# Attention and a mixture-of-experts layer: in each expert's turn GpSimd issues the adds into the output ahead of the fetches of rank rows for the next expert

## The reference

```python
x = x + _L0_xattn_ref(_layernorm(x), ctx_1024, Wq, Wk, Wv, Wp, bp)     # 16 heads of 16
x = x + _L0_ffn_ref(_layernorm(x), ...)

# _L0_ffn_ref, cut: 8192 tokens, E = 16 experts, F = 1024, capacity 512 tokens per expert
xn = xf / rms * norm_weight
logits = xn @ router_weight.T + router_bias
probs = softmax(logits, axis=-1)
_, idx = top_k(logits.T, 512)                  # each expert picks its own 512 tokens
xe = xn[idx]
h = gelu(einsum('ecd,efd->ecf', xe, fc1_weight) + fc1_bias[:, None, :])
y = einsum('ecf,edf->ecd', h, fc2_weight) + fc2_bias[:, None, :]
gates = take_along_axis(probs.T, idx, axis=1)
output = zeros.at[flat_idx].add(y * gates[:, :, None])
gate_sums = zeros.at[flat_idx].add(gates)
output = where(gate_sums > 0, output / gate_sums, output)
```

## Time and profile before

| what | value |
|---|---|
| median of 3 runs | 1093.96 us (1087.89 to 1103.24) |
| profiled execution | 1097.2 us, its span 1095.2 us |
| PE busy | 886.7 us (81%) |
| DVE busy | 767.9 us (70%) |
| POOL busy | 645.6 us (59%) |
| ACT busy | 498.9 us (46%) |
| mean granted TensorE clock | 0.904 of full |

### The profile page before, as it was taken

The page is one execution under the profiler, slowest core; times in us unless marked ns, Lnnn a source line. Parts: engine busy times, 40 slices in busy tenths (PEclk is TensorE's granted clock), DMA queues, the critical chain, the costliest instruction groups (busy, mean ns, idle before and its releaser), DMA issues.

```text
span 1095.2 us, 20141 instructions
## 1 busy us (share of the span) xinstructions
PE 886.7 (81%) x6006; PEld 703.1 (64%) x6006; DVE 767.9 (70%) x1539; ACT 498.9 (46%) x868; POOL 645.6 (59%) x617
## 2 busy tenths in 40 slices
PE   4899999999999999997400015999999899989975
PEld 3566666766677666664400014888878798978874
DVE  4668888888888888875399885576666667676541
ACT  1446555556555565554100004564655544445440
POOL 3246655656656566553630055578887788888624
PEclk9889999999999999998555557999999999999996
DMA  4345555555565555552300052155555555555523
GB/s 157 134 143 186 194 209 210 186 207 189 192 218 192 196 199 184 212 213 99 109 0 0 0 156 85 39 134 141 152 157 149 134 133 129 134 137 131 125 63 38
DMA packets 110819, 155.17 MB, mean 142 GB/s; under 512 B 21180, under 2 KB 78780, under 8 KB 110784
## 3 DMA queue, kind: packets, MB, share of 16 engines
q1 hardware_dynamic: 94400, 133.71, 35.4%
q0 software_dynamic: 16384, 21.02, 10.8%
HBM read 61.86 MB, written 26.21 MB: 80 GB/s over the span
## 4 chain that ended last, share of the span: by engine, by line
PE 12%; DVE 11%; DMA 9%; issue 9%; POOL 8%; ACT 1%; SPq 0%; DVEq 0%; POOLq 0%; ACTq 0%
DMA W<-w1T_dram 4%; PE bank L1388 4%; PE bank L1389 4%; PE bank L1390 4%; DMA XG<-xn_table,II 3%; POOL XG L1075 2%; POOL out_dram L1101 2%; POOL RK L1069 2%; POOL G L1081 1%; DVE junk L883 1%; DVE before L1176 1%; DVE W2L L1221 1%; ACT W1H L1338 1%; DMA RK<-rank_table,RI 1%; DVE cand L893 1%
## 5 line engine op out<-in xcount | busy, mean ns | idle before, releaser
L525 DVE TENSOR_REDUCE NM<-bank 128x4 f32<-128x480 f32 x256 | 159.6, 656 | 53.7 <-PE bank L635 53.3
L368 ACT ACTIVATE PT<-bank 120x512 f32<-120x512 f32 x256 | 139.1, 595 | 64.4 <-PE bank L660 63.6
L310 POOL TENSOR_SCALAR XN<-X,mv,rstd 128x256 f32<-128x256 f32 x128 | 155.7, 1224 | 6.9 <-POOL rstd L305 6.1
L1388 PE MATMUL bank<-W2H,HH 128*128 128x256 f32 x512 | 147.5, 288 | 5.7 <-DVE Y L1261 5.7
L1389 PE MATMUL bank<-W2L,HH 128*128 128x256 f32 x512 | 145.9, 285 | 0.0
L1390 PE MATMUL bank<-W2H,HL 128*128 128x256 f32 x512 | 145.8, 285 | 0.0
L1247 DVE TENSOR_TENSOR HL<-HF,HH 128x512 fp32r<-128x512 f32 x128 | 87.0, 692 | 75.0 <-ACT HH L1351 74.8
L1101 POOL DMA_INDIRECT out_dram<-C,IO x60 | 112.1, 1868 | 45.0 <-DVE C L1266 27.3
L1388 PE MATMUL bank<-XTH,W1H 128*128 128x512 f32 x256 | 105.2, 411 | 18.7 <-DVE XTL L1231 18.7
L343 POOL TENSOR_TENSOR XB<-X,bp_sb 128x512 f32<-128x512 f32 x32 | 40.5, 1266 | 123.4 <-DVE X L536 123.4
L478 DVE RECIPROCAL RR<-RC 128x256 f32<-128x256 f32 x64 | 111.2, 1741 | 1.5 <-DMA RC<-PVS 1.5
(11 more groups left out here) (148 smaller groups left out, 1773.4 us busy)
## 6 DMA issues: line engine op xcount, KB each, us to landing
QX<-QH SPq DMA_DIRECT2D x64, 256.0 KB
W<-w1T_dram SPq DMA_DIRECT2D x16, 1024.0 KB
W<-w2T_dram SPq DMA_DIRECT2D x16, 1024.0 KB
KX<-KH SPq DMA_DIRECT2D x64, 240.0 KB, 2.3
X<-x_dram SPq DMA_DIRECT2D x32, 256.0 KB, 2.8
QX<-QL SPq DMA_DIRECT2D x32, 256.0 KB
RC<-PVS SPq DMA_DIRECT2D x32, 256.0 KB, 2.4
OC<-PVS SPq DMA_DIRECT2D x32, 256.0 KB, 2.6
```

The lines of the kernel that those rows point to most:

```text
L310: ins = pool.tensor_scalar(dst[:, t, :], src[:, t, :], mv[:, t, 0:1], rstd[:, t:t + 1], ALU.subtract, ALU.mult)
L368: act.activation(PT[u][0:M, HE * k:HE * (k + 1), :], score_bank[k % 2][0:M, :], ACT.Exp, scale=SCALE) \
L525: dve.tensor_reduce(NM[u][:, t, :].rearrange("p (f n e) -> p n e f", n=HN, e=HE)[:, n, :, :], smax_bank[q % 2][:, 0:4 * M].rearrange("p (e ...
L1388: pe.matmul(o, wh, xh, start=first, stop=False)
```

## The change

In both halves of GpSimd's loop the call of `add_up` changes place with the call of `ranks`. The loop's contents, its semaphores and the code before and behind it stay as they are.

```diff
@@ -1123,11 +1123,11 @@
         ranks(1, 1, RI[1])
         with pool.Fori(1, E // 2 - 1) as i:
             gather(i, 1)
+            add_up(i - 1, 0, False)
             ranks(i + 1, 0, RI[0])
-            add_up(i - 1, 0, False)
             gather(i + 1, 0)
+            add_up(i - 1, 1, False)
             ranks(i + 1, 1, RI[1])
-            add_up(i - 1, 1, False)
         gather(E // 2 - 1, 1)
         add_up(E // 2 - 2, 0, False)
         add_up(E // 2 - 2, 1, False)
```

## The result

The changed kernel took 1165.16 us (median of 4 runs, 1159.88 to 1166.56) against 1093.72 us (4 runs) before: ratio 1.0635, 95% interval 1.0552 to 1.0718. Two later comparisons of the same pair, on chips 4 and 5, gave 1.0474 (1.0411 to 1.0537) and, with more executions, 1.0584 (1.0558 to 1.0610). It is slower by 5 to 6%. The ratios leave out the few executions that ran over 1.5% above the fastest of their kernel. The forecast was 1139 us; the profiled execution took 1165.9 us, its span is 1163.9 us.

A forecast was written before the change was run, and what follows sets the result against it. GpSimd's queue was taken as the bound, TensorE close behind. Twelve waits of 3.7 us less 0.7 gave 43.7; plus 3.1, less 2.14 in the tail, 44.7, taken as +45: 1139 us, range 1117 to 1172.

The forecast's parts named there:

- forecast case: Likeliest case, each turn exposing the wait for rank rows: +45 us, 1139 us, own range 1126 to 1152, chance 0.72.
- rank rows that land late: Rival: rank rows take up to 8.2 us instead of 2.5; 1207 us, or 1162 in one turn of three; chance 0.12.
- GpSimd's queue bounds the turn: In the expert phase, GpSimd's 16 transfers a turn sum to 25.3 us against turns of 25.67; TensorE next at 24.3.
- The exposed chain: Rank fetch landing 2.48, `find` 1.59, GpSimd's reaction 0.90: 4.97 us, against 1.25 without a wait; new wait 3.7 a turn.
- the row of the phase's start: Expert phase's start, where VectorE really waited for rank rows: fetch issued at 646.11 us, `find` at 648.59, so 2.48 us.
- Twelve turns: Token fetches of experts 4 to 15 each follow a rank fetch directly: 12 x 3.7 - 0.7 = 43.7 us.
- the stretching: Lengthening of GpSimd instructions beside W1L, priced as unchanged when W1L meets rank fetches instead of adds.
- My layout: Predicted new turn, laid out from the first token fetch, to check that VectorE is free when rank rows land.
- G + 6.8: Time in us after G, the turn's first token fetch, near which W2L was predicted to end.
- The tail: After the last token fetch: 3.1 us later since `find` of expert 15 loses its lead, less a vanished 2.14 us wait.
- The clock: Rival: 5 us TensorE pauses slow first-layer matmuls, losing 10 us a turn; TensorE becomes the bound, 1199 us; chance 0.06.
- hidden: Rival, not slower: TensorE sets the pace, GpSimd's durations are only stretched, so the edit is hidden; 1094 us, chance 0.10.

The follow-up runs named there:

- The shortened HL: VectorE's HL subtraction done on 64 of 512 columns: changed kernel 1168.97 us, ratio 1.0494 to the kernel before; same edit in the kernel before 1114.18 us.

## Why the prediction was right, and where it was too small

The direction, the mechanism and its place were right, and the time is inside the range; the size was 71 us against 45 in the first comparison, 54 and 64 in the others. That the range held is in part luck. The forecast case's own range was 1126 to 1152 us, and 1165 lies above it; the upper bound of 1172 had been drawn for rank rows that land late, which did not happen. Of the 24 us between the spans' 68.7 and the forecast 44.7, 16.8 lie in the turns (60.5 against 43.7), 6.2 ahead of expert 3 and 0.9 in the tail.

- *GpSimd's queue bounds the turn.* Shown by leaving out gate fetches: the same move then costs 2.6 us.
- *The exposed chain.* Priced at 2.48 + 1.59 + 0.90 = 4.97 us, measured 2.58 + 1.70 + 0.84 = 5.12. The estimate of 2.15 us for the landing by DMA: Bandwidth & Descriptors, section Anatomy of one DMA, of the Trainium skill was too low here, counted from the start of GpSimd's instruction; the row of the phase's start was near.
- *Twelve turns.* Right; `find` waited 12 times, and half of the moves cost half.
- *"W1L now meets rank fetches on GpSimd where it met adds; I price the stretching at the same."* This is the term that was mis-sized. Turns grew by 5.05 us, not 3.7: 3.9 of it is the wait over the usual 0.3 us and 1.1 is longer instructions, which the prediction took as unchanged. Before, GpSimd's queue ran free of VectorE, and its turns took 24.1 to 27.2 us. W1L met an add and W2L a token or gate fetch, now early in the split and now late. In the changed kernel everything restarts at `find`, so the splits fall on the same instruction each time: W2L starts at 869.32, half a microsecond ahead of the first gate fetch (2.60 us instead of 0.95), W1L at 884.39, ahead of the first rank fetch (2.57). That is so in all twelve turns. My layout had W2L end at G + 6.8 and W1L start at G + 19.5; both came true within 0.1 us (871.61 and 884.39 are G + 6.8 and G + 19.55). I had the positions and did not price what they hit. The price was to be read in the kernel before, where an add that began 0.33 us into a W1L took 3.40 us, not 1.6:

```profile
902.56 2.29 DVE L1215 TENSOR_TENSOR W1L<-W,W1H 128x2048 fp32r<-128x2048 f32 x1 [3.36 <-ACT W1H L1338]
...
902.89 3.40 POOL L1101 DMA_INDIRECT out_dram<-C,IO  x1 [0.30 <-issue]
```

From the durations over the twelve turns, set against 0.95 us for a fetch and 1.6 for an add, my estimate is that the two large splits lengthen GpSimd's instructions by 2.5 us a turn before and 3.3 after, 0.8 of the 1.1. The adds now also lie beside the HL subtractions. That GpSimd and VectorE contend in VectorE's instructions with two inputs in SBUF is what the Trainium skill says in GPSIMD Engine Reference, Key points. The shortened HL agrees for the short subtractions. For W1L and W2L no run here took them away, but the ends of the lengthened instructions agree (last section).
- *The tail.* Forecast 1.0 us longer from the last token fetch (44.7 - 43.7), measured 1.9.
- *The rest of the first comparison.* 6.2 us ahead of expert 3's token fetch is not the change: 5.45 of it lies in unchanged code, and in the second pair that part was 6.8 us shorter in the changed kernel. Without it the first pair of profiles differs by 62 us.
- *Rivals.* Rank rows landed in 2.6 us, not late. The clock did fall after each pause, as TensorE: Matmul & The Clock Gate of the Trainium skill, section HAM oscillation, says of a kernel that waits for transfers in every turn, and as that rival said. But it lengthened TensorE's turn by 1.7 us, not by the 10 of that rival, and 26.0 us still fitted into 30.7. The change was not hidden.

No variant beat the kernel before with the whole computation. Leaving out gate fetches shows what is to be had from relieving GpSimd: 1.3%.

## What to carry to other kernels

When an engine's queue is full, its order is a place to hide latency: before two items are swapped, look for a round trip through another engine between an item and its successor, and price it from the one place where it is already exposed. When a new wait locks engines together, averages of contended durations no longer hold; lay out which instruction the neighbour's long ones will meet, and use its worst case. A pause on an engine with 5 us of room can cost its clock and still cost no time.

## What the runs showed of the hardware that was not expected

- GpSimd's indirect fetch of 0.94 us takes 2.6 us if it starts 0.5 us after the start of a 2.29 us VectorE subtraction of 128x2048, turn after turn. What counts is the end of the subtraction. In the profiles of both kernels every fetch that began inside such a subtraction, 0.16 to 1.14 us after its start, ended 0.81 to 0.90 us after the subtraction's end, and every add that did (0.14 to 1.80 us after the start) ended 1.43 to 1.49 us after it. An instruction that was already running when the subtraction began was not made longer: the add at 876.09 us in the earlier trace rows took 1.62 us beside a W1L that began at 876.39. The subtraction took its 2.29 us either way.
- After a TensorE pause of 4.7 us the granted clock was 0.51 over 866 to 872 us, and 1.00 over the next 6 us. It was as low after each of the twelve pauses, and the twelve cost TensorE 20 us of busy time in all and the kernel none.
- The unchanged part of the kernel ahead of the experts ended at times 10 us apart in profiled executions (628.59 to 638.62 us for the same instruction).
